# Two-layer graph network on one Trainium2 core: means and score rows by way of memory, and a shifted schedule for unit 7, unit 4 and two row sums

## What is computed

```python
h = jnp.maximum(_layernorm(x), 0.0)
# layer 0: two propagations through T
Xw = X @ Wv + bv
sj = Xw @ aw[:d, 0]; si = Xw @ aw[d:, 0]
e = leaky_relu(sj[:, None, :] + si[:, :, None] + ab[0], 0.2)
alpha = A * jnp.exp(e)
T = alpha / (jnp.sum(alpha, axis=-1, keepdims=True) + 1e-12)
H = X @ Wk[0] + (T @ X) @ Wk[1] + (T @ T @ X) @ Wk[2] + biases
x = x + relu(H)
h = jnp.maximum(_layernorm(x), 0.0)
# layer 1
Ah = A + I; dh = rsqrt(sum(Ah, -1))
x = x + relu((dh * Ah * dh.T) @ h @ kernel + bias)
```

## Time and profile before

| | |
|---|---|
| median of 3 runs | 774.48 us (774.38 to 774.57) |
| the profiled execution | 775.14 us, its span 772.9 us |
| instructions | 14177 |
| granted TensorE clock | 0.998 over the span |

### The profile page before, as it was taken

How to read it: one execution, slowest core, us unless ns; L and a number is a source line. 1 busy time by engine, 2 the same in 40 slices (tenths; PEclk the granted TensorE clock), 3 DMA queues, 4 the chain that set the end, 5 groups by cost and what they waited for, 6 DMA issues and landing times.

```text
span 772.9 us, 14177 instructions
## 1 busy us (share of the span) xinstructions
PE 758.8 (98%) x5190; PEld 695.6 (90%) x5190; DVE 610.9 (79%) x1420; ACT 539.6 (70%) x1051; POOL 183.9 (24%) x184
## 2 busy tenths in 40 slices
PE   8699999999999999999999999999999999999997
PEld 8498988989899898998989989899998989889986
DVE  6986888778896789967888678886888777895665
ACT  3988797567966679657785578856698567976351
POOL 1031240312403123130321405123050321402330
PEclk9999999999999999999999999999999999999999
DMA  6846339624497055970569505784148733356411
GB/s 226 298 137 193 120 132 320 225 96 137 138 317 263 20 154 177 299 243 1 177 208 302 187 13 184 255 272 150 69 144 303 240 118 109 133 209 210 140 62 54
DMA packets 60660, 135.93 MB, mean 176 GB/s; under 512 B 6320, under 2 KB 32304, under 8 KB 60592
## 3 DMA queue, kind: packets, MB, share of 16 engines
q1 hardware_dynamic: 51824, 104.35, 41.1%
q10 hardware_dynamic: 8768, 30.68, 11.4%
HBM read 126.62 MB, written 8.39 MB: 175 GB/s over the span
## 4 chain that ended last, share of the span: by engine, by line
PE 90%; DVE 4%; ACT 4%; issue 1%; DMA 1%; SPq 0%; DVEq 0%
PE acc L1132 16%; PE acc L1134 16%; PE acc L1133 16%; PE da L992 11%; PE db L992 6%; PE da L1102 4%; PE da L1100 4%; PE da L1101 4%; PE tp L1100 4%; PE tp L1102 4%; PE tp L1101 4%; ACT tg_e L471 2%; PE acc L1023 1%; ACT g_hi L439 1%; PE tp L1010 1%
## 5 line engine op out<-in xcount | busy, mean ns | idle before, releaser
L1132 PE MATMUL acc<-g_hi,t_hi 128*128 128x256 f32 (+1 forms) x1024 | 291.9, 285 | 2.8 <-DVE g_lo L721 2.8
L1134 PE MATMUL acc<-g_hi,t_lo 128*128 128x256 f32 (+1 forms) x1024 | 290.3, 284 | 0.0
L1133 PE MATMUL acc<-g_lo,t_hi 128*128 128x256 f32 x1024 | 289.6, 283 | 0.0
L1132 PEld LDWEIGHTS acc<-g_hi,t_hi 128*128 128x128 f32 x1024 | 194.1, 190 | 3.5 <-issue 3.2
L1133 PEld LDWEIGHTS acc<-g_lo,t_hi 128*128 128x128 f32 x1024 | 194.6, 190 | 0.3
L1134 PEld LDWEIGHTS acc<-g_hi,t_lo 128*128 128x128 f32 x1024 | 194.5, 190 | 0.0
L366 POOL TENSOR_TENSOR g_lo<-tmp,g_hi 128x256 fp32r<-128x256 f32 x64 | 58.6, 916 | 265.8 <-ACT g_hi L524 265.8
L471 ACT ACTIVATE tg_e<-si,sij 128x256 f32<-128x256 f32 x256 | 109.3, 501 | 4.0 <-DVE sij L708 4.0
L758 DVE TENSOR_TENSOR a_lo<-a_raw,a_hi 128x512 fp32r<-128x512 f32 x128 | 89.7, 720 | 25.1 <-ACT a_hi L514 25.1
L361 POOL TENSOR_TENSOR rstd<-ve,mhalf 128x2 f32<-128x2 f32 (+2 forms) x41 | 51.3, 1251 | 193.6 <-DVE ve L658 144.9
L524 ACT CAST g_hi<-tmp 128x256 fp32r<-128x256 f32 x64 | 25.9, 404 | 101.1 <-DVE tmp L772 101.1
(11 more groups left out here) (146 smaller groups left out, 1635.0 us busy)
## 6 DMA issues: line engine op xcount, KB each, us to landing
a_raw<-adj_dram SPq DMA_DIRECT2D x64, 512.0 KB, 4.6
a_raw<-adj_z_dram SPq DMA_DIRECT2D x64, 512.0 KB, 3.9
tg_a<-adj_t_dram ACTq DMA_DIRECT2D x58, 512.0 KB, 4.4
x_o<-x_dram SPq DMA_DIRECT2D x64, 128.0 KB, 2.5
out_dram<-x_o SPq DMA_DIRECT2D x64, 128.0 KB, 3.5
x_nat<-x_dram SPq DMA_DIRECT2D x28, 256.0 KB, 4.3
xt<-x_t_dram SPq DMA_DIRECT2D x28, 256.0 KB, 4.5
tg_a<-adj_t_dram SPq DMA_DIRECT2D x6, 512.0 KB, 4.0
```

The lines of the kernel that those rows point to most:

```text
L1132: nc.tensor.matmul(acc[:, s, 0:n], l_hi, r_hi, start=(jt == 0), stop=False)
L1133: nc.tensor.matmul(acc[:, s, 0:D], l_hi, r_lo, start=False, stop=False)
L1134: ins = nc.tensor.matmul(acc[:, s, 0:n], l_lo, r_hi, start=False, stop=(jt == NT - 1))
```

## The change

- `rows_of_mean`: instead of eight transposes of a mean column spread over 128 columns, one transpose of the 8 columns of `mv0` gives 8 rows of 128. It stands in the middle of chunk 3 of the first propagation (chunk 2 for the first batch). ScalarE copies it to SBUF (`mean_copy`), SP writes it to a new DRAM tensor, waits for it, and reads it back to all 128 partitions into `si` (`mean_over_partitions`), 512 KB in SBUF. `centre` reads `si`.
- `si_turned`: two transposes of 4 columns each instead of eight of one: one behind tile 4 of the dense stage, one in the middle of chunk 0 of the second propagation; copy, write, wait and read as above (`si_over_partitions`, 256 KB each), issued by SP in front of residual load 2.
- Leaky relu and exp of unit 0 move from behind the tiles 4 and 5 of the dense stage to behind tile 7, its product from behind tile 6 to behind tile 7.
- Unit 7 is made in the batch's own first propagation: leaky relu and exp behind chunk 0, product, high and low part behind 1, 2, 3.
- Product 4 moves from behind chunk 7 of the second propagation to behind piece 0 of the layer 1 stage; product 1 and high part 1 move one chunk on.
- Row sums 6 and 7 move into the dense stage, behind tiles 0 and 1. The statistics of the next x stand behind chunks 0 and 1 instead of 0 to 3.

```diff
-    SCORE_V = {-1: 1, 2: 2, 3: 3, 5: 4}
-    HIGH_V = {1: (0, 1), 5: (2,)}
-    PROD_V = {0: 1, 3: 2, 5: 3, 7: 4}
+    SCORE_V = {0: 1, 2: 2, 3: 3, 5: 4}
+    HIGH_V = {1: (0,), 2: (1,), 5: (2,)}
+    PROD_V = {1: 1, 3: 2, 5: 3}
...
+    LEAKY_Z, EXP_Z = {4: 5, 9: 6}, {5: 5, 10: 6}
+    HIGH_Z, HIGH_U = {0: 3, 6: 4, 11: 5, 14: 6}, {2: 7}
+    PROD_Z, PROD_U = {0: 4, 5: 5, 11: 6}, {1: 7}
+    LOW_Z, LOW_U = {1: 3, 7: 4, 12: 5, 15: 6}, {3: 7}
...
+    ROWS_U, ROWS_D = {0: (0,), 1: (1,), 2: (2,), 3: (3,), 4: (4,), 5: (5,)}, {0: (6,), 1: (7,)}
...
+            def mean_over_partitions(b):
+
+                sp.wait_ge(mean_t_ready, b)
+                sp.dma_start(mean_dram, mean_t).then_inc(mean_stored, 16)
+                sp.wait_ge(mean_stored, 16 * b)
+
+                sp.wait_ge(leaky_done, b * NU)
+                sp.dma_start(si[:, :], mean_dram.rearrange("t (o p) -> o (t p)", o=1).to_broadcast([P, N])).then_inc(mean_loaded, 16)
...
+                if b == 0 and u % 2 == 0:
+
+                    act.wait_ge(si_ready, u // 2 + 1)
+                elif b > 0 and u % HJ == 0:
+
+                    act.wait_ge(si_loaded[u // HJ], 16 * b)
...
                 dve.wait_ge(xt_loaded[g], 16 * b)
-                dve.wait_ge(mean_full, 2 * (b - 1) + g // 2 + 1)
-                row = mean_rows[g // 2][:, g % 2 * 2 * P:(g % 2 + 1) * 2 * P]
+                dve.wait_ge(mean_loaded, 16 * b)
+                row = si[:, g * 2 * P:(g + 1) * 2 * P]
...
+                nc.tensor.transpose(mean_bank, mv0[:, :, 0], ident[:, :]).then_inc(mean_full, 1)
...
+            def si_turned(b, h):
+
+                if h == 0:
+
+                    pe.wait_ge(g1_tmp_ready, b * NT)
+                else:
+                    pe.wait_ge(si_t_ready, 2 * b - 1)
+                pe.wait_ge(p0_ready, b * NT + HJ * (h + 1))
+                nc.tensor.transpose(si_bank, sij[:, h * HJ:(h + 1) * HJ, 1], ident[:, :]).then_inc(si_t_full, 1)
```

More of the change, by code:

```diff
@@ L377, in batch @@
                     g1_split(b, i)
-                    if i == (3 if b > 0 else -1) and not last:
+                    if i == (1 if b > 0 else -1) and not last:
                         power(rstd0, ve0, ve0_ready, b + 1, rstd0_ready)
@@ L519, in batch @@
                         zt_high(b - 1, 1)
+                    if i == (2 if b == 0 else 3) and not last:
+                        mean_copy(b + 1)
                     if i >= NT - 2 and not last:
@@ L533, in after @@
                 def after(t):
[L534 removed]
+                    for r in (FIRST_ROWS_D if b == 0 else ROWS_D).get(t, ()):
                         rows(b, r)
@@ L539, in after @@
                         a_round(b, 0, 1)
-                    if t == 4 and not last:
-                        leaky(b + 1, 0)
-                    if t == 5 and not last:
-                        exponent(b + 1, 0)
                     if t == 6:
@@ L547, in after @@
                         a_round(b, 1, 1)
+                        if not last:
+                            leaky(b + 1, 0)
+                            exponent(b + 1, 0)
                 if not last:
@@ L829, in batch @@
                     u_chunk(b, i)
+                    if not last and b > 0:
+                        for t in STATS_U.get(i, ()):
+                            stats0_of(b + 1, t)
+                        if i == 1:
+                            moments0(b + 1)
                     if i in (NT - 3, NT - 2) and not last:
@@ L838, in batch @@
                         t_low(b, low[i])
[L839 to L843 removed]
                 def after(t):
[L845 removed]
+                    if t == 5:
                         dve.wait_ge(rows_done, b * NT + NT)
@@ L855, in after @@
                         diag(b, 1)
-                    if t == 6 and not last:
-                        t_prod(b + 1, 0)
                     if t == 7:
@@ L860, in after @@
                         a_low(b, 1, 1)
+                        if not last:
+                            t_prod(b + 1, 0)
                 if not last:
@@ L1116, in out_product, with accumulate @@
                                                     for f in range(KD)]).then_inc(out_full, 1)
-            def accumulate(b, phase, i, read, before, ready, n, rhs):
+            def accumulate(b, phase, i, read, before, ready, n, rhs, middle=None):
                 s = acc_slot(phase, i)
@@ L1127, in accumulate @@
                 for jt in range(NT):
+                    if jt == HJ and middle is not None:
+                        middle()
                     if ready is not None and i == 0:
```

93 lines of the change are left out of this document (42 added, 51 removed).

## The result

The changed kernel takes **778.95 us** (778.58 to 779.53, 4 runs) against 774.43 us of the kernel before in the same comparison: ratio 1.0062, 95% interval 1.0049 to 1.0074. It is slower by 0.6%, 4.5 us, and lies outside the predicted range of 764.6 to 776.5; the forecast was 768.9. The time of each run is the median of its executions near the full clock (0.98 and more over the span); one execution of the kernel before with product 4 moved, which took 1052.2 us at a granted clock of 0.655, is left out.

The account below looks back on a forecast made before the run. TensorE, hardly ever waiting after start-up, was taken as the bound. Terms of -5.3, -2.4 and +2.1 sum to -5.6: 775.14 becomes 769.5 us profiled, 768.9 us as median; range 764.6 to 776.5.

Parts of the forecast that it names:

- Term 1: First propagation: one mean transpose instead of eight saves 0.76 us in each of 7 stages, 5.3 us in all.
- Term 2: Dense stage: fewer score transposes, less some waits, shorten it from 18.24 to 17.9 us, saving 2.4 us in all.
- Term 3: Score and mean rows' trip through memory: both land in time and cost nothing, the scores with 0.8 us of slack.
- Term 4: Layer 1 stage: moving units 0 and 4 makes TensorE wait 0.3 us before the seventh piece, 2.1 us lost in all.
- B: Rival, chance 0.15: no wait in the layer 1 stage, 766.8 us, or 764.6 with a dense saving of 4.6.
- C: Rival, chance 0.14: dense stage stays chain-bound and saves nothing, new layer 1 wait is 0.75 us, 774.5 us.
- D: Rival, chance 0.19: score rows land late, delaying leaky relu 0 by 1.4 us; layer 1 wait 1.7 us, 778.7 us.

Follow-up runs that it names:

- the means alone: Kernel before with only the single mean transpose, mean row through memory and statistics in chunks 0 and 1: 773.94 us, ratio 1.0002.
- the run with the row sums back: Changed kernel with product 4 behind piece 1, low parts 3 and 4 behind pieces 4 and 8, row sums 6 and 7 back in first propagation: 791.59 us.

## Why the prediction was wrong

**Term 1, the means (-5.3): right.** First propagations 25.96, 0.76 shorter. What the prediction did not see is that this hangs on the row sums' move (the means alone gave nothing). It wrote that behind the blocked SyncE stand "only residual loads", which is true of the scores' trip and was not asked of the means'. By the figure of the Trainium skill ("TensorE: Matmul & The Clock Gate", Back-to-back issue gap) the term would have been an estimated 4.0; by the windows, the row's 0.76 per stage held.

**Term 2, the dense stage (-2.4): right in size** (17.87 against 17.9), mixed in reason. Unit 0's move alone, with all transposes in place, gave 17.97: most of the gain is ScalarE's room. The row sums cost 0.1, not the waits I had listed.

**Term 3, the memory way (0): right.** Write to read 1.17 us for the scores (I had said 2.4) and 2.3 for the means, reads 3.2 and 4.5 median against 3.5 and 4 to 4.6 said. The scores' read went out at 169.96 and landed near 173.2; leaky relu 0 wanted them at 175.52, so the slack was 2.3 us, not 0.8 (and its own figures, 6.5 + 0.9 - 6.4, give 1.0):

```profile
175.52 1.71 ACT L511 ACTIVATE tg_e<-si,sij 128x256 f32<-128x256 f32 x4
```

The centring waits 0.5 for the mean row in the batch shown, at no cost.

**Term 4 is the step that failed**: 0.3 us per batch (2.1 in all, bound 8.4) was 1.85 (13.0). The prediction had the right mechanism, place and releaser, and its chain up to the bias held within 0.4 (measured, then said): last moments V+27.1 (said 26.7), GpSimd's low parts V+27.1 (27.2), power 1.08 (0.7 to 0.9), product 4 at V+28.41 (28.2). The power took more than the 0.7 to 0.9 said because VectorE isn't quiet there: an adjacency low part stands at 201.84 (it is in the order that the section on the change shows), and the power ends 0.55 behind it. Then the prediction added 1.12, 0.66, 1.15 and 0.69, the lengths of instructions for which VectorE doesn't have to wait. GpSimd's low parts of the fourth pair, started by the same bias, begin ahead of the last two, which took 1.68 to the next start and 1.22: 1.06 us that no term held. The ready time was V+33.06, not V+31.8: 0.23 from the later bias, 1.06 from the contention, the rest rounding. TensorE wanted it at V+31.35, not 31.5; two restarts and the eighth piece make up the last tenths. The bound failed in the same way: it varied the power and left the rest fixed. The rows to see it were at hand: the three low parts of the kernel before from 206.49 take 2.44 us, in which one is 1.23.

**What the netting hid.** The lag of unit 0 had no term of its own: the prediction followed it to the bias and set it off against the shorter power that product 4's move allows ("V+28.1, as now"). With both edits made, that held within 0.4 (the bias ends at V+28.46). But it made the lag look free. Each edit alone adds 1.1 us to the ready time, and the slack against which they stand, 0.71 us, was never written down.

**Rivals.** B and C named the wrong number for the layer 1 stage. D's time (778.7) is almost the measured one, by a mechanism that did not act: a right number is no proof of its cause. Slower had been given a chance of 0.18.

## What to carry to other kernels

When an operation is moved behind a synchronising value (here the bias), every engine that the value starts is busy in that moment: take the durations for the moved work from rows in which the other engine is busy too, and see which of the two starts first, since here the second one paid. Compute for each queue the one time that matters, ready minus wanted, before and after; slack that two edits share is spent once. And edits of one change may only pay together: ask for each what it does if the others were missing, and where a value that was moved is read (the row sums' addition on VectorE).

## What the hardware showed that I had not expected

- Subtractions of two SBUF operands take turns across VectorE and GpSimd: the one that starts second is the long one, and on VectorE it ends 0.55 us (128x512) or 1.08 us (128x1024) behind the end of GpSimd's. On VectorE 1.22 becomes 1.76 and 0.68 becomes 1.22; on GpSimd the state's low part takes 0.74 alone and 1.71 behind unit 3's. Moving one GpSimd instruction moved the slow row with it. Products of unit 4 that start ahead of GpSimd's power keep 1.21 to 1.23, while the power itself takes 1.61 instead of 0.69.
- Behind a wait of 2.79 us TensorE's granted clock was 0.50 (1.2 GHz) from 41.18 to 43.18 in one profiled execution and 1.00 in another; in the run with the row sums back it was 0.86 to 0.93 on average in four dense stages, behind waits of 1.8 to 3.1, and 1.00 in two, behind waits of 2.8 and 2.9. The length of the wait alone didn't decide it.
- A 2 KB write to memory, waited for, costs 1.17 us, five in a row 5.8. A 4 KB write took 1.2 us (the means alone) to 2.3 (the changed kernel) at the same place of the program.
- Some 7.4 MB more in 776 us, and the median adjacency load lands in 5.7 us where it took 4.6. Whether volume or position does it was not tried.
